# Moving the state update, D times x and the dt scale of an SSD scan between engines, in an 8-core layer kernel

## The reference

```python
x = x + 0.5 * ffn(layernorm(x), sign, scale)      # x @ sign * softplus(scale)
x = x + attn(layernorm(x), ...)
x = x + 0.5 * ffn(layernorm(x), sign, scale)
# attn: gate, hBC, dt = split(hidden @ in_proj_w.T); hBC = silu(conv4(hBC)); dt = softplus(dt + dt_bias)
A_dt = -exp(A_log) * dt;  x_dt = x * dt            # x, B, C from hBC
A_cumsum = cumsum(A_dt within the chunk)
Lmat = exp(segment_sum(A_dt))                      # exp(a_l - a_s) for s <= l, else 0
Y_diag = ((C B^T) * Lmat) @ x_dt                   # within a chunk
states = (B * exp(a_last - a))^T @ x_dt            # one state per head and chunk
new_state = exp(a_last) * state + states           # carried over the chunks
Y_off = C @ state * exp(a)
y = Y_diag + Y_off + D * x
y = y * rsqrt(mean(y^2) + eps) * norm_w * silu(gate)
return y @ out_proj_w.T
```

## Time and profile before

| | us |
|---|---|
| median of 2 runs | 13,149.94 |
| the two runs | 12,876.5 and 13,423.37 |
| the profiled execution | 12,875.27 |
| its span, slowest core (core 0) | 12,873.7 |
| spans of the eight cores | 12,841.4 to 12,873.7 |

### The profile page before, as it was taken

One profiled execution on the slowest core, in us unless ns is written; L12 is line 12 of the kernel. 1 busy time (PEld: TensorE's weight loads), 2 busy tenths in 40 slices (PEclk: granted clock), 3 DMA queues, 4 the chain that ended last, 5 costly groups with the idle time before them and its releaser, 6 DMA issues. The chain is left out here.

```text
span 12873.7 us, 116458 instructions; the slowest of 8 cores (12841.4 to 12873.7 us)
## 1 busy us (share of the span) xinstructions
PE 9247.7 (72%) x46264; PEld 4509.7 (35%) x46264; DVE 3888.4 (30%) x3914; ACT 1238.9 (10%) x1078; POOL 272.5 (2%) x359
## 2 busy tenths in 40 slices
PE   3799379999999999962342433424328997993799
PEld 0344034444444444431232322323213443440344
DVE  4200420000133333333564655646540000004200
ACT  2000200000000000001222222222210000002000
POOL 0000000000000000000000000000000000000000
PEclk6899589999999999985555555555559998995899
DMA  4443433323323323320111111111125545444443
GB/s 175 126 117 104 176 82 58 59 55 59 58 56 59 58 56 59 59 53 9 40 23 40 26 28 38 22 41 25 28 55 121 115 108 131 111 109 176 126 118 105
DMA packets 751546, 986.35 MB, mean 77 GB/s; under 512 B 639906, under 2 KB 640034, under 8 KB 674850
## 3 DMA queue, kind: packets, MB, share of 16 engines
q0 software_dynamic: 59024, 428.89, 17.9%
q1 hardware_dynamic: 489236, 407.32, 10.4%
q10 hardware_dynamic: 202752, 142.70, 3.4%
HBM read 1120.16 MB, written 211.82 MB: 103 GB/s over the span
## 5 line engine op out<-in xcount | busy, mean ns | idle before, releaser
L65 PE MATMUL psW<-xlnAB,wbp 128*128 128x512 bf16 x18560 | 4008.7, 379 | 170.1 <-DMA wbp<-WinB 170.1
L65 PEld LDWEIGHTS psW<-xlnAB,wbp 128*128 128x128 bf16 x18560 | 1816.6, 98 | 2362.6 <-issue 174.5
L65 PE MATMUL psD<-ygh,wob 128*128 128x512 bf16 x8192 | 1773.2, 380 | 304.9 <-DMA ygh<-ygs 304.9
L65 PEld LDWEIGHTS psD<-ygh,wob 128*128 128x128 bf16 x8192 | 802.5, 98 | 1275.3 <-issue 312.0
L65 PE MATMUL psFfa<-xlnAB,sgfa 128*128 128x512 bf16 x4096 | 886.4, 380 | 177.9 <-DMA sgfa<-SgB 177.9
L65 PE MATMUL psFfe<-xlnE,sgfe 128*128 128x512 bf16 x4096 | 886.9, 380 | 175.7 <-DMA sgfe<-SgB 175.7
L72 PE MATMUL psSt<-identF,sdf 128*128 128x128 f32 x16 | 7.1, 446 | 1303.0 <-ACT decf L46 1303.0
L46 DVE TENSOR_TENSOR x2t<-psD,xrd 128x1024 f32<-128x1024 f32 x64 | 78.4, 1225 | 1928.6 <-PE psD L65 1928.6
L46 DVE CAST gev<-psW 128x2048 bf16<-128x2048 f32 x64 | 146.7, 2292 | 1635.9 <-PE psW L65 1635.9
L65 PEld LDWEIGHTS psFfa<-xlnAB,sgfa 128*128 128x128 bf16 x4096 | 401.3, 98 | 663.4 <-issue 181.7
L65 PEld LDWEIGHTS psFfe<-xlnE,sgfe 128*128 128x128 bf16 x4096 | 401.4, 98 | 661.6 <-issue 180.1
(11 more groups left out here) (172 smaller groups left out, 6204.6 us busy)
## 6 DMA issues: line engine op xcount, KB each, us to landing
wbp<-WinB POOLq DMA_DIRECT2D x145, 1024.0 KB, 8.0
wob<-WoutB POOLq DMA_DIRECT2D x64, 2048.0 KB, 15.7
xfa<-x0T SPq DMA_DIRECT2D x64, 1024.0 KB, 4.8
xfb<-x1s SPq DMA_DIRECT2D x64, 1024.0 KB, 4.9
xfe<-x2s SPq DMA_DIRECT2D x64, 1024.0 KB, 4.9
xcs<-xev ACTq DMA_DIRECT2D x1280, 32.0 KB, 1.6
xcb<-xcs POOLq DMA_DIRECT2D x16, 2560.0 KB, 17.5
xrfa<-x0T SPq DMA_DIRECT2D x32, 1024.0 KB, 13.6
```

What stands on the lines that cost most here:

```text
L65: inst = self.e.matmul(out, lhsT, rhs, start=start, stop=stop, **kw)
```

## The change

In the scan:

- The logarithm of dt, also split in two bf16 parts (`lnhb`, `lnlb`), becomes a fifth and sixth row of psL, so that Lex holds exp(a_l - a_s) times dt. xdt is then x itself: a ScalarE copy of psT behind Lex. xdd is xdt times `ddtT` (dt times decay).
- `dgb`: VectorE writes into rtmp four diagonal matrices, identF times dexpA. Four f32 matmuls (`recmm`) of these with Ssb add to psSt. ScalarE copies psSt to Ssb (`rec`) and psYc to Ybf (`yev`) for the round before.
- D times x is multiplied and added to Ybf on VectorE ahead of y2st (`dadd`), 1,024 columns at a time.
- The load of xcb for chunk c + 1 waits for the last ygst of chunk c - 1 (`yg`).
- The prelude gets one Ln, four VectorE instructions and two stores per chunk.

In the layer norm, the loads of odd tiles are issued by POOL instead of SP.

The diff, cut to its core:

```diff
@@ pool_stream
                 if c >= 1:
                     p.wait(S["pe"], M["rnd_end", c - 1])
-                    p.wait(S["dve"], M["yev", c - 1, 15])
+                    p.wait(S["dve"], M["yg", c - 1, 7])
@@ sync_stream
-            k = s.dma(bncB[3, off:off + 128 * CS].rearrange("(p l) -> p l", p=128), albf[:], bnc)
+            s.dma(bncB[3, off:off + 128 * CS].rearrange("(p l) -> p l", p=128), albf[:], bnc)
+            s.dma(bncB[4, off:off + 128 * CS].rearrange("(p l) -> p l", p=128), lnhb[:], bnc)
+            k = s.dma(bncB[5, off:off + 128 * CS].rearrange("(p l) -> p l", p=128), lnlb[:], bnc)
...
                 s.dma(lhsT4[0:2, :], bncB[0:2, off:off + 4096], rla)
+                s.dma(lhsT4[4:6, :], bncB[4:6, off:off + 4096], rla)
                 k = s.dma(rhs4[2:4, :], bncB[2:4, off:off + 4096], rla)
@@ pe_stream
                 p.wait(S["dve"], M["msb", c, r])
+                p.wait(S["act"], M["xdt", c, r])
                 for hh in range(8):
...
                 if rec: M["smm", c, r] = k
+                p.wait(S["dve"], M["dgb", c, r])
+                if c >= 1:
+                    p.wait(S["act"], M["rec", c - 1, r])
+                for j in range(4):
+                    k = p.mm(psSt[r % 2][:, j * 128:(j + 1) * 128],
+                             rtmp[:, j * 128:(j + 1) * 128],
+                             Ssb[:, r * 512 + j * 128:r * 512 + (j + 1) * 128],
+                             False, True, skip_group_check=True, mark=(j == 3))
+                if rec: M["recmm", c, r] = k
@@ dve_stream
+            d.wait(S["act"], M["preln", c])
+            km = d.op("tensor_copy", lnhb[:], ln32[:], dep=km)
+            km = d.op("tensor_copy", ah32[:], lnhb[:], dep=km)
+            km = d.op("tensor_tensor", al32[:], ln32[:], ah32[:], ALU.subtract, dep=km)
+            k = d.op("tensor_copy", lnlb[:], al32[:], dep=km)
...
-            def rec_yev(r):
...
             for r in range(16):
+                if r >= 1:
+                    p_recmm = M["recmm", c, r - 1]
...
+                d.wait(S["pe"], p_recmm)
+                k = d.op("tensor_tensor", rtmp[:].rearrange("p (a b) -> p a b", a=4),
+                     identF[:].unsqueeze(1).to_broadcast((128, 4, 128)),
+                     dexpA[:, c * 64 + r * 4:c * 64 + r * 4 + 4].unsqueeze(2).to_broadcast((128, 4, 128)),
+                     ALU.mult,
+                     dep=M["dgb", c, r - 1] if r >= 1 else (M["dgb", c - 1, 15] if c >= 1 else None))
+                if rec: M["dgb", c, r] = k
...
-                d.wait(S["pe"], M["xtr", c, r])
-                k = d.op("tensor_tensor", xdt[r % 2][:].rearrange("p (a b) -> p a b", a=8),
-                         psT[0][:, 0:512].rearrange("p (a b) -> p a b", a=8),
-                         dtT[:, r * 8:r * 8 + 8].unsqueeze(2).to_broadcast((128, 8, 64)), ALU.mult,
-                         dep=M["xdd", c, r - 2] if r >= 2 else None)
...
+                d.wait(S["act"], M["xdt", c, r])
                 k = d.op("tensor_tensor", xdd[r % 2][:].rearrange("p (a b) -> p a b", a=8),
                          xdt[r % 2][:].rearrange("p (a b) -> p a b", a=8),
-                         decayT[:, r * 8:r * 8 + 8].unsqueeze(2).to_broadcast((128, 8, 64)), ALU.mult,
-                         dep=M["xdt", c, r])
+                         ddtT[:, r * 8:r * 8 + 8].unsqueeze(2).to_broadcast((128, 8, 64)), ALU.mult,
+                         dep=M["xdd", c, r - 2] if r >= 2 else None)
...
-                if r >= 1:
-                    rec_yev(r - 1)
-            rec_yev(15)
             for gr in range(8):
...
+                d.wait(S["act"], M["yev", c, 2 * gr + 1])
+                km = d.op("tensor_tensor", t1st[gr % 2][:].rearrange("p (a b) -> p a b", a=8),
+                          xcb[c % 2][:, gr * 1024:(gr + 1) * 1024].rearrange("p (a b) -> p a b", a=8),
+                          Dex[:, gr * 8:gr * 8 + 8].unsqueeze(2).to_broadcast((128, 8, 128)), ALU.mult,
+                          dep=M["dadd", c, gr - 2] if gr >= 2 else (M["yg", c - 1, 6 + gr] if c >= 1 else None))
+                km = d.op("tensor_tensor", Ybf[:, gr * 1024:(gr + 1) * 1024],
+                          Ybf[:, gr * 1024:(gr + 1) * 1024], t1st[gr % 2][:], ALU.add, dep=km)
+                if rec: M["dadd", c, gr] = km
@@ act_stream, prelude
+            k = a.op("activation", ln32[:], dtv[:, c * CS:(c + 1) * CS], AF.Ln,
+                     bias=cons[:, 14:15], dep=None)
@@ act_stream, round r, behind Lex
+                a.wait(S["pe"], M["xtr", c, r])
+                if r >= 2:
+                    a.wait(S["dve"], M["xdd", c, r - 2])
+                k = a.op("activation", xdt[r % 2][:], psT[0][:, 0:512], AF.Copy,
+                         dep=None)
...
+                if r >= 1:
+                    a.wait(S["pe"], M["ydiag", c, r - 1])
+                    k = a.op("activation", Ybf[:, (r - 1) * 512:r * 512], psY[(r - 1) % 2][:, :],
+                             AF.Copy, dep=None)
...
+                    a.wait(S["pe"], M["recmm", c, r - 1])
+                    k = a.op("activation", Ssb[:, (r - 1) * 512:r * 512], psSt[(r - 1) % 2][:, :],
+                             AF.Copy, dep=None)
@@ ln_phase, first pass (the second is changed in the same way)
             @blk.sync
             def _(sy):
                 s = Eng(sy, None)
-                for dc in range(NDC):
+                for dc in range(0, NDC, 2):
                     if dc >= 2:
                         s.wait(S["pe"], mmstm(dc - 2))
-                    ldm[dc] = s.dma(xf[dc % 2][:], src[dc], ldx[dc % 2])
+                    ldm[dc] = s.dma(xf[0][:], src[dc], ldx[0])
+
+            @blk.gpsimd
+            def _(sy):
+                s = Eng(sy, None)
+                for dc in range(1, NDC, 2):
+                    if dc >= 2:
+                        s.wait(S["pe"], mmstm(dc - 2))
+                    ldm[dc] = s.dma(xf[1][:], src[dc], ldx[1])
```

More of the change, by code:

```diff
@@ L231, in pe_stream @@
             if c >= 1:
-                p.wait(S["dve"], M["yev", c - 1, 15])
+                p.wait(S["act"], M["yev", c - 1, 15])
             for g in range(8):
@@ L284, in pe_stream @@
                 if r >= 1:
-                    p.wait(S["dve"], M["xdtc", c, r - 1])
+                    p.wait(S["act"], M["xdtc", c, r - 1])
                 else:
@@ L293, in pe_stream @@
                 if r >= 2:
-                    p.wait(S["dve"], M["yev", c, r - 2])
+                    p.wait(S["act"], M["yev", c, r - 2])
                 if r == 0:
@@ L326, in pe_stream @@
                 elif r == 1:
[L327 removed]
+                    p.wait(S["act"], M["rec", c - 1, 15] if c >= 1 else 0)
                 else:
[L329 removed]
+                    p.wait(S["act"], M["rec", c, r - 2])
                 g = r // 2
@@ L416, in dve_stream @@
             if rec: M["btev", c] = k
-            def rec_yev(r):
[L418 to L422, removed]
-                     dep=M["yev", c, r - 1] if r >= 1 else (M["yev", c - 1, 15] if c >= 1 else None))
-                k = d.op("tensor_tensor", Ssb[:, r * 512:(r + 1) * 512], rtmp[:], psSt[r % 2][:, :],
-                         ALU.add, dep=km)
-                if rec: M["rec", c, r] = k
-                d.wait(S["pe"], M["ydiag", c, r])
-                km = d.op("tensor_tensor", rtmp[:].rearrange("p (a b) -> p a b", a=4),
-                     xcb[c % 2][:, r * 512:(r + 1) * 512].rearrange("p (a b) -> p a b", a=4),
-                     Dex[:, r * 4:r * 4 + 4].unsqueeze(2).to_broadcast((128, 4, 128)), ALU.mult,
-                     dep=M["rec", c, r])
-                k = d.op("tensor_tensor", Ybf[:, r * 512:(r + 1) * 512], psY[r % 2][:, :],
-                         rtmp[:], ALU.add, dep=km)
-                if rec: M["yev", c, r] = k
-            for r in range(16):
+            for r in range(16):
+                if r >= 1:
+                    p_recmm = M["recmm", c, r - 1]
+                elif c >= 1:
+                    p_recmm = M["recmm", c - 1, 15]
+                else:
+                    p_recmm = 0
+                d.wait(S["pe"], p_recmm)
[5 more added lines that the diff above has]
+                if rec: M["dgb", c, r] = k
                 if c >= 1:
@@ L544, in act_stream @@
             for sg in range(8):
-                a.wait(S["dve"], M["rec", c, 2 * sg + 1])
                 if sg >= 1:
@@ L835, in _ @@
                 s = Eng(sy, None)
-                for dc in range(NDC):
+                for dc in range(0, NDC, 2):
                     if dc >= 2:
                         s.wait(S["dve"], aplm(dc - 2))
-                    ldm[(1, dc)] = s.dma(xf[dc % 2][:], src[dc], ldx[dc % 2])
+                    ldm[(1, dc)] = s.dma(xf[0][:], src[dc], ldx[0])
+            @blk.gpsimd
+            def _(sy):
+                s = Eng(sy, None)
+                for dc in range(1, NDC, 2):
+                    if dc >= 2:
+                        s.wait(S["dve"], aplm(dc - 2))
```

(1 more changed line is left out.)

49 lines of the change are left out of this document (29 added, 20 removed).

## The result

| us | before | after |
|---|---|---|
| median | 13,338.35 (10 runs, 12,876.5 to 14,085.88) | 13,995.03 (11 runs, 13,590.29 to 14,740.78) |
| the profiled execution | 12,875.27 | 13,608.95 |
| its span | 12,873.7 (core 0) | 13,607.4 (core 6) |
| granted clock, mean | 0.80 | 0.80 |

The change makes the kernel slower: the ratio is 1.0558, 95% interval [1.0534, 1.0582]. In most executions of either kernel the cores of one die ran at a lower clock and took some per cent longer; the ratio leaves these out, while both medians hold them and so lie above the profiled executions.

A forecast was written before the change was run, and what follows sets the result against it. No engine was full; a ring of hand-overs through three engines was taken to bound the rounds. 713 + 19 + 14 - 57 + 50 + 0 = 739 on 12,875 gave 13,614 us, own range 13,440 to 13,870.

The forecast's parts named there:

- the term for the layer norm loads: Layer norms: odd tiles loaded by POOL gain nothing, 0; rival that POOL's loads are slow, +288 us, chance 0.08.
- the wide range: Whole kernel: 13,400 to 14,100 us, leaving out the clock and the busiest engine.
- the forecast's own range: Whole kernel: 13,440 to 13,870 us around 13,614, chance 0.62.
- the f32 price: State matmuls in the rounds: 0.22 us per f32 instruction, 1.76 per round; rival 0.46 each, +432 us, chance 0.16.
- The ring: Scan rounds: hand-overs through TensorE, ScalarE and VectorE set the round, 5.96 us growing to 8.93, +713 us.
- the clock rises: Rival, scan rounds: longer TensorE stretch brings 2.4 GHz, ring's TensorE terms halve, -504 us to 13,110; chance 0.09.
- The tail: Behind each chunk's rounds: D times x moved there makes y2st's spacing 2.72 us instead of 2.02, +14 us.
- The load of xcb: Output loop loses 11.1 us in 14 chunks, next chunk's first psL comes 7 later: -57 us, between -141 and +13.
- The prelude: Two more stores ahead of dlc's in 16 turns, 1.56 us each: +50 us, bounds +14 and +182.
- the busiest engine sets the round: Rival, scan rounds: ring not closed, TensorE's 5.6 us replaces 5.96, -86 us, total 12,796 us; chance 0.05.

The follow-up runs named there:

- e1: The changed kernel with each round's four state matmuls issued behind psL of the next round: rounds 6.86 us apart, cores 4 to 7 took 13,112 to 13,141 us.
- e2: The changed kernel with Msb ahead of xdd on VectorE: rounds 7.75 us apart, cores 0 to 3 took 13,318 to 13,356 us.
- e7: The changed kernel with three of each round's four state matmuls left out: rounds 7.64 us apart, cores 4 to 7 took 13,259 to 13,291 us.

## Why the prediction was right or wrong

Two steps failed: the base of the sum, 12,875 us, for a kernel whose median came out at 13,338, and the term for the layer norm loads, 0, which measured +93 to +99 us. The mechanism of the rounds, 91% of the change, was right.

**The direction and its cause: right.** No engine was the bound, a ring over three engines was, and the change put two things on it. e1, e2 and e7 (the state update later, Msb first, one state matmul) each took one of them, or part of one, off. Against 8.76 the first two got 1.90 and 1.01 us back, of which 1.5 and 1.0 at an unchanged clock of 1.2 GHz; the third, against 8.90, got 1.26 back for six instructions.

**The figure.** I wrote "I forecast against the lower one", and so gave 13,614 for what turned out as 13,995. Against the execution that the sum was made for it is 13,614 to 13,609, and 13,614/12,875 = 1.057 stands against the measured 1.0558. The step that failed is the choice of base: two runs 4% apart had shown that a median would lie above the lower one, and the kernel before itself came out at 13,338. The ratio is what the working can give; the medians add 2.8% (after) and 3.6% (before) that no term of the sum stands for. That 13,995 lies in the wide range is luck: it is over the forecast's own range (to 13,870) and is covered only by bounds that were put there for rivals that didn't come, the f32 price above all.

**The ring: right, +2.97 forecast, +2.94 in a round at 1.2 GHz** (8.90 against 5.96). Its terms erred a little against each other: 1.26 from Lex's end to Msb where I had 1.45, because ScalarE starts xdt 0.1 us before Lex ends and xdd follows xdt's end by 0.17 instead of 0.24; 1.81 for the eight f32 instructions where I had 1.76; and 0.94 from Msb's start to psYc's, where I had left the 0.83 of before, for which I have no cause. The mean over all rounds is 8.76, +2.78, as the clock rose at times: +671 instead of +713. The rival "the clock rises" had 0.09 and came in part, 34 us of its 504.

**The f32 price: right.** 0.21 to 0.23 per instruction at 1.2 GHz, as the 128-column transposes had it; the 64-column pair was not set by its columns. (The rival's sum had a slip: 8 x 0.46 - 1.76 is 1.9 us and not 1.8, so +461 and not +432.)

**The tail: right**, +13.8 for +14; the spacing of y2st is the 2.72 of the sum.

**The load of xcb: right in kind, mis-sized.** -57 forecast, about -97 measured. The head took 5.9 us a chunk, not 7; the loop gave 12.9, not 11.1. The step "the load costs 11.1 us" took for its measure a chunk without the load, the fifteenth, whose output loop still held a gate load at its end:

```profile
9362.67 1.15 POOL L51 DMA_DIRECT2D gtb<-gates  x1 [18.27 <-ACT sgst L46]
...
9368.77 1.23 DVE L46 TENSOR_TENSOR t1st<-Ybf,RSTD 128x1024 bf16<-128x1024 bf16 x1 [7.84 <-DMA ygs<-ygst]
```

In POOL's queue that gate load stands behind xcb's, so the moved wait took it out of the loop as well, and the last spacing of t1st fell from 11.0 to 8.3 us. The trace of before bears this out: with no load of xcb in either, this spacing is 11.19 in the fifteenth chunk, with the gate load, and 8.67 in the sixteenth, without it. The first wait of psL grew to 7.36 us, where I had "near 9".

**The prelude: mis-sized**, +50 forecast, +21 as the mean of eight cores. albf's landing stayed near its place (4.8 us after issue, before 5.2), and the two new stores landed after 5.0 and 5.5, dlc's after 11.4 instead of 10.5. So stores behind one another overlap, and nearly only SP's issues count: the lower bound, 14, was nearer. A turn grew by 1.3 us, not 3. Between traces of one and the same prelude the mean of the eight cores varies, from 240 to 253 us in three traces of the old one and from 248 to 272 in nine of the new one, so this term isn't known to better than some 10 us.

**The layer norms: the step of the mechanism that failed.** "Two are not asked for at one time, so a second queue has nothing to overlap: I take 0" was right on overlap (the run with ScalarE's queue shows it) and left out that the issuer changes. POOL issues 0.4 us later, its loads land 0.4 to 1.2 us later (medians of the three layer norms), and the second pass has no slack. That is +93 to +99, 13% of the loss. The upper bound, +288 from 3 us per load, had the right mechanism at nearly three times its size; it stood in the range at 0.08 and should have been a term of the sum. These 93 hid the errors of the other side (42 in the rounds, 40 at the load, 29 in the prelude), which is why the sum looks better than its terms.

**The rival on the other side**, "the busiest engine sets the round", named its condition, psL of the next round ahead of the wait for Msb. Made true in before, it gives -128 us; made true in after, together with Msb ahead of xdd, Zsb ahead of the diagonal, a second rtmp and SP's loads, it turns a loss of 5.6% into a gain of over 4%. Its price of -86 took TensorE's 5.6 us at 1.2 GHz as the bound; with after's ring open the clock rises and ScalarE's 3.75 us is the bound, so the rounds take 901 us, 526 less than in before. That rival was mis-sized because I left the clock where the closed ring kept it.

Open: why the state update issued late is worth 1.5 us at 1.2 GHz and not its 1.81, what makes POOL's loads late, and which of the edits in the fastest kernel carries how much.

## What to carry to other kernels

Read busy shares in the stage that repeats, not over the whole; and where no engine is full there, write out the ring of hand-overs and ask of each moved instruction whether it stands on it: work taken from VectorE was worth nothing here, and 3 us put on the ring cost 671. Before balancing engines, issue the next round's first step ahead of this round's wait; here the balance paid only with that, and the clock rose with it. And forecast a ratio: a median of two runs that lie 4% apart is no base for a sum made from one trace.

## What the runs showed that I had not expected

- The mean granted clock of the rounds took many values between the two levels: 0.50 (before, one state matmul, ring open in before), 0.57 (after), 0.60 (Msb first), 0.66 (state late), 0.85 (filler in before), 0.94 (ring open in after), 0.97 (filler in after).
- Filler work paid where the gap was longer than it, 8.76 to 7.10 us in after, and not on the mean in before, where rounds of 5.58 us at 2.4 GHz stand beside rounds of 7.54 at 1.2.
- A round of 3.75 us in which ScalarE's instructions overlap by 0.1 us where they don't depend on one another.
- The same load of 1,024 KB lands 4.7 to 5.1 us after SP's issue and 5.5 to 5.9 after POOL's; from ScalarE's queue it is as quick as from SP's.
